# Mixture-of-experts layer: token rows and addresses straight from the tables, scaling parameters on VectorE, and each row gather behind the tile's additions on GpSimd

## The reference

```python
xn = rms_w * (x * rsqrt(mean(x * x) + EPS))
gate_w = softmax(xn @ wg_W + wg_b + (cond @ gg_W + gg_b))
topk_w, topk_i = top_k(gate_w, 2)
cw = sum(one_hot(topk_i, 8) * topk_w[..., None], axis=-2)
h1 = relu(x @ W1[e] + b1[e]); h2 = relu(h1 @ W2[e] + b2[e])
out = x + sum_e cw[..., e] * (h2 @ W3[e] + b3[e])
```

## Time and profile before

| | us |
|---|---|
| median of three runs | 458.6 |
| the profiled execution's own time | 455.86 |
| its span, first to last instruction | 454.2 |
| PE busy | 410.7 |
| POOL busy | 314.9 |
| DVE busy | 304.7 |
| ACT busy | 291.2 |

### The profile page before, as it was taken

One profiled execution on the slowest core, in us unless ns is written; L12 is line 12 of the kernel. 1 busy time (PEld: TensorE's weight loads), 2 busy tenths in 40 slices (PEclk: granted clock), 3 DMA queues, 4 the chain that ended last, 5 costly groups with the idle time before them and its releaser, 6 DMA issues.

```text
span 454.2 us, 12827 instructions
## 1 busy us (share of the span) xinstructions
PE 410.7 (90%) x4110; PEld 365.2 (80%) x4110; DVE 304.7 (67%) x539; ACT 291.2 (64%) x617; POOL 314.9 (69%) x457
## 2 busy tenths in 40 slices
PE   8705989979999989989989989989999999999993
PEld 6505978868888878878878878878888899988892
DVE  4799774858858748748747748655566677776661
ACT  6704959869779668859758855545545556565542
POOL 5631861778678878878778778778878776654534
PEclk9955899999999999999999999999999999999999
DMA  8999289677736737435437435536455444512322
GB/s 299 335 262 338 108 286 375 178 163 189 184 60 165 180 66 168 76 58 78 84 55 183 76 58 81 86 54 105 89 80 86 87 73 71 72 39 36 48 30 31
DMA packets 60968, 57.82 MB, mean 127 GB/s; under 512 B 42059, under 2 KB 55437, under 8 KB 58733
## 3 DMA queue, kind: packets, MB, share of 16 engines
q1 hardware_dynamic: 43072, 38.85, 29.6%
q0 software_dynamic: 13632, 18.00, 24.4%
q10 hardware_dynamic: 4205, 0.17, 0.5%
HBM read 40.08 MB, written 17.83 MB: 128 GB/s over the span
## 4 chain that ended last, share of the span: by engine, by line
POOL 31%; PE 24%; issue 18%; DMA 9%; DVE 6%; POOLq 5%; ACT 5%; SPq 2%; DVEq 1%; ACTq 0%
PE bank L1373 17%; POOL out L688 11%; PE y_banks L1456 5%; POOL area L653 4%; POOL cw L676 3%; DMA out<-in_x 3%; POOL cfrom L648 3%; DMA out<-area,cto 3%; POOLq L664 2%; ACT area L858 2%; POOLq L674 2%; DMA stage<-in_weights 2%; PE bank L1353 2%; POOL cto L648 1%; ACT w_hi L764 1%
## 5 line engine op out<-in xcount | busy, mean ns | idle before, releaser
L1373 PE MATMUL bank<-area,w_hi 128*128 128x256 f16 x1296 | 214.5, 273 | 8.1 <-DVE area L1158 6.6
L1373 PE MATMUL bank<-area,w_lo 128*128 128x256 f16 x648 | 176.6, 273 | 0.0
L872 ACT ACTIVATE area<-bank,cprm 128x256 f32<-128x256 f32 (+1 forms) x264 | 129.4, 558 | 51.3 <-PE bank L1373 32.3
L688 POOL DMA_INDIRECT out<-area,cto x71 | 122.0, 1718 | 44.5 <-issue 15.6
L1156 DVE CAST area<-area 128x512 f16<-128x512 f32 (+1 forms) x144 | 67.2, 467 | 118.3 <-ACT area L872 109.8
L1373 PEld LDWEIGHTS bank<-area,w_hi 128*128 (+1 forms) x1296 | 125.9, 98 | 24.6 <-issue 10.1
L1158 DVE TENSOR_TENSOR area<-area 128x512 f16<-128x512 f32 (+1 forms) x144 | 100.7, 699 | 4.9
L1456 PE MATMUL y_banks<-w_hi,area 128*128 (+1 forms) x520 | 90.8, 273 | 5.5 <-DVE area L1158 5.3
L653 POOL DMA_INDIRECT area<-x_ext,cfrom x65 | 68.2, 1050 | 37.8 <-POOL cfrom L648 28.0
L884 ACT ACTIVATE area<-area,cw 128x256 f32<-128x256 f32 x71 | 32.2, 499 | 65.3 <-DVE area L1163 42.0
L1456 PE MATMUL y_banks<-w_lo,area 128*128 (+1 forms) x260 | 70.9, 273 | 0.0
(11 more groups left out here) (216 smaller groups left out, 504.6 us busy)
## 6 DMA issues: line engine op xcount, KB each, us to landing
stage<-in_weights SPq DMA_DIRECT2D x10, 1024.0 KB, 5.3
area<-in_x SPq DMA_DIRECT2D x8, 512.0 KB, 7.1
x_ext<-in_x SPq DMA_DIRECT2D x8, 512.0 KB
out<-in_x SPq DMA_DIRECT2D x8, 512.0 KB, 10.2
w_lo<-in_weights SPq DMA_DIRECT2D x4, 1024.0 KB, 6.7
w_hi<-in_weights SPq DMA_DIRECT2D x2, 1024.0 KB
out<-area,cto POOLq DMA_INDIRECT x71
area<-x_ext,cfrom POOLq DMA_INDIRECT x65, 3.4
```

What stands on the lines that cost most here:

```text
L688: pool.indirect_dma_start(out=out, out_offset=bass.IndirectOffsetOnAxis(ap=cto[:, s, u:u + 1].bitcast(U32), axis=0), in_=yb[:, s, u, :], i ...
L872: ins = act.activation(to[:, m * T + u * wide:m * T + (u + 1) * wide], ps_h[layer][b][:, a * T + u * wide:a * T + (u + 1) * wide], ACT.Rel ...
L1373: ins = nc.tensor.matmul(out_m, weight, moving, start=(k == 0 and n == 0), stop=(k == chunks - 1 and n == 2))
```

## The change

1. POOL's `copy_columns` is gone: gathers read their offsets from `tab_from`, additions theirs from `tab_to`, with no copy and no wait for one.
2. `parameters(e)` is moved from POOL to DVE, with 12 instructions in place of 14, behind `finish(i)` and `low_parts` of the same steps; rank 0's stands before `x_low(0)`. POOL waits for it through `s_params`.
3. In POOL's turn `gather_into` stands behind `add_rows(i)`, and `copy_weights` stays ahead.
4. At the start POOL issues the gathers of tiles 0 and 1 before it waits for rank 0's parameters; PE transposes tile 1's rows ahead of `layer2(0)`, with 16 filling matmuls in place of 24; ACT's `x_high(1)` stands before `squares(3)`; DVE's `x_low(1)` stands before the second `low_parts(0)`, and `experts_of_tiles` inside step 0, behind its two splits.
5. `low_parts` of chunks 2 and 3 stand in DVE's steps 0 and 1 (before: 1 and 2), behind `finish`; the loads of chunks 8 and 9 follow a step earlier.

```diff
-LOWS_AT, SQUARES_AT, SUMS_AT, HIGHS_AT, PARAMETERS_AT = {1: 2, 2: 3}, {}, {0: 1}, {0: 2, 1: 3}, {0: 1}
+LOWS_AT, SQUARES_AT, SUMS_AT, HIGHS_AT, PARAMETERS_AT = {0: 2, 1: 3}, {}, {0: 1}, {0: 2, 1: 3}, {0: 1}
...
+        def last_rank(i):
+            return 0 if i < FIRST else min(i * E // LEAST, E - 1)
...
-            def copy_columns(to, table, i, signal):
-                pool.tensor_copy(to, table[:, bass.ds(i * SUB, SUB)]).then_inc(signal, 1)
...
+            def gather(i):
+                s = i % RING
                 for u in range(halves_of(i)):
+                    rows = tab_from[:, i * SUB + u:i * SUB + u + 1]
...
             def copy_parameters(i, s):
                 experts = []
+                pool.wait_ge(s_params, last_rank(i) + 1)
...
             def gather_into(n):
-                s = n % RING
                 wait_free(n - RING)
-                copy_columns(cfrom[:, s, :], tab_from, n, s_cfrom)
-                pool.wait_ge(s_cfrom, n - RING + 1)
+                pool.wait_ge(s_cw, n - RING + 1)
                 pool.sem_inc(s_own, 1)
-                gather(n, s, cfrom[:, s, :])
+                gather(n)
...
-            def step(i, s, first=False, late=None, next2=True):
-                copy_columns(cto[:, s, :], tab_to, i, s_idx)
+            def step(i, s, first=False, next2=True):
                 if next2 and i > 1:
                     copy_weights(i + 2, (s + 2) % RING, experts_of[i + 2])
-                for n in GATHERS_AT.get(i, ()):
-                    gather_into(n)
-                pool.wait_ge(s_idx, i + 1)
...
                 add_rows(i, s)
                 if by_halves(i):
                     next_parameters(i, s)
+                for n in GATHERS_AT.get(i, ()):
+                    gather_into(n)
                 if i < 2:
                     copy_weights(i + 2, (s + 2) % RING, experts_of[i + 2])
-                if late is not None:
-                    link(parameters(late))
...
             for i in range(RING):
-                gather(i, i, tab_from[:, i * SUB:(i + 1) * SUB])
-                if i == 0:
-                    pool.wait_ge(s_whole, 1)
-                    pool.wait_ge(s_order, 1)
-                    link(parameters(0))
+                if i == RING - 1:
                     experts_of.append(copy_parameters(0, 0))
+                gather(i)
...
+            def parameters(e, label):
+                dve.wait_ge(s_wsc, e + 1)
+                dve.wait_ge(s_whole, 1)
+                dve.wait_ge(s_b3[e], 16)
+                link(dve.scalar_tensor_tensor(one, w1_sq, xmax4, whole[:, bass.ds(label, 1)], ALU.mult, ALU.add))
+                link(dve.scalar_tensor_tensor(two, one, w2_sq, whole[:, bass.ds(label + E, 1)], ALU.mult, ALU.add))
...
+                ins.then_inc(s_params, 1)
```

More of the change, by code:

```diff
@@ L118 @@
 FLOOR_P = 1.5 * 2.0 ** 23 * P
+WHOLE = 1.5 * 2.0 ** 23
 QUAD = 4
@@ L580, in _ @@
             ins.then_inc(s_iota, 1)
[L582 to L606, removed]
             def inverse_rms(c):
@@ L645, in wait_free @@
                 pool.wait_ge(s_xp if i < BY_PE else s_xs, i + 1)
-            def copy_columns(to, table, i, signal):
-                pool.tensor_copy(to, table[:, bass.ds(i * SUB, SUB)]).then_inc(signal, 1)
-            def gather(i, s, rows):
+            def gather(i):
+                s = i % RING
                 for u in range(halves_of(i)):
+                    rows = tab_from[:, i * SUB + u:i * SUB + u + 1]
                     pool.indirect_dma_start(
                         out=xg[:, s, u, :], out_offset=None, in_=x_ext,
-                        in_offset=bass.IndirectOffsetOnAxis(ap=rows[:, u:u + 1].bitcast(U32), axis=0),
+                        in_offset=bass.IndirectOffsetOnAxis(ap=rows.bitcast(U32), axis=0),
                     ).then_inc(s_xg[s], 16)
@@ L688, in add_rows @@
                     pool.indirect_dma_start(
-                        out=out, out_offset=bass.IndirectOffsetOnAxis(ap=cto[:, s, u:u + 1].bitcast(U32), axis=0),
+                        out=out, out_offset=bass.IndirectOffsetOnAxis(
+                            ap=tab_to[:, i * SUB + u:i * SUB + u + 1].bitcast(U32), axis=0),
                         in_=yb[:, s, u, :], in_offset=None, bounds_check=N - 1, oob_is_err=False,
@@ L750, in _ @@
             for i in range(TILES):
-                step(i, i % RING, first=(i == 0), late=PARAMETERS_AT.get(i),
-                     next2=i + 2 < TILES)
+                step(i, i % RING, first=(i == 0), next2=i + 2 < TILES)
             pool.wait_ge(s_add, MOST * 16)
@@ L910, in _ @@
             activate(0, 0, 0)
+            x_high(1)
             squares(3)
-            x_high(1)
             for i in range(TILES):
@@ L1191, in step @@
                     split(i + 1, 0)
+                if i == 0:
+                    experts_of_tiles()
                 if next1 and two(i) and two(i + 1):
@@ L1204, in step @@
                     copy_weights(LAST, 0, i - AFTER)
-                if late is not None:
+                if late is not None and i >= FRONT:
                     low_parts(late)
@@ L1210, in step, with label_of @@
                     finish(i, s)
+                if late is not None and i < FRONT:
+                    low_parts(late)
+                if i in PARAMETERS_AT:
+                    parameters(PARAMETERS_AT[i], label_of(PARAMETERS_AT[i]))
+            def label_of(e):
+                return dve.value_load(order[0:1, e:e + 1], min_val=0, max_val=E - 1)
+            def parameters(e, label):
+                one, two = bound[:, e, 0:1], bound[:, e, 1:2]
+                w1_sq, w2_sq = fsq[:, e, 0:1], fsq[:, e, 2:3]
+                c1, c2, c3 = (prm[:, e, c:c + 1] for c in range(3))
+                s1, s3, s2, sh1, sh2 = (scale[:, e, c:c + 1] for c in range(5))
+                inv_s1, inv_s3, inv_s2, inv_sh1, inv_sh2 = (inv_scale[:, e, c:c + 1] for c in range(5))
+                dve.wait_ge(s_wsc, e + 1)
[3 more added lines that the diff above has]
+                link(dve.scalar_tensor_tensor(two, one, w2_sq, whole[:, bass.ds(label + E, 1)], ALU.mult, ALU.add))
+                link(dve.tensor_scalar(bound[:, e, :], bound[:, e, :].bitcast(I32), -0.5 * 2.0 ** -MANT, 1.5 * BIAS,
+                                       ALU.mult, ALU.add))
+                link(dve.tensor_scalar(expo[:, e, 3:5], bound[:, e, :], WHOLE, WHOLE, ALU.add, ALU.subtract))
+                dve.tensor_scalar(scale[:, e, 3:5].bitcast(I32), expo[:, e, 3:5], float(TOP_LOG), 2.0 ** MANT,
+                                  ALU.add, ALU.mult)
+                link(dve.tensor_scalar(inv_scale[:, e, :].bitcast(I32), expo[:, e, :], -2.0 ** MANT,
+                                       (2.0 * BIAS - TOP_LOG) * 2.0 ** MANT, ALU.mult, ALU.add))
+                dve.scalar_tensor_tensor(c1, sh1, inv_sx, inv_s1, ALU.mult, ALU.mult)
+                dve.scalar_tensor_tensor(c2, sh2, inv_sh1, inv_s2, ALU.mult, ALU.mult)
+                dve.tensor_tensor(c3, inv_sh2, inv_s3, ALU.mult)
+                for at, sh in ((0, sh1), (KM, sh2)):
+                    ins = dve.tensor_tensor(prm[:, e, 4 + at:4 + at + KM],
+                                            packed[:, bass.ds(label * (2 * KM) + (KH + KH * E + at), KM)],
+                                            sh.to_broadcast([P, KM]), ALU.mult)
+                ins.then_inc(s_params, 1)
@@ L1212, in _ @@
             dve.wait_ge(s_sx, 1)
             dve.sem_inc(s_y32, 1)
+            first_label = label_of(0)
             low_parts(0, (0,))
+            parameters(0, first_label)
             x_low(0)
@@ L1217, in _ @@
             split(0, 0)
+            x_low(1)
             low_parts(0, (1,))
-            x_low(1)
             tables()
-            experts_of_tiles()
             for i in range(TILES):
```

11 lines of the change are left out of this document (4 added, 7 removed).

## The result

The changed kernel takes 460.35 us (median of 20 runs, 458.89 to 464.36) beside 457.55 for the kernel before (20 runs, 447.72 to 461.0): 2.8 us or 0.6% more. The ratio reported for this comparison is 1.0219, interval 1.0162 to 1.0276; it rests on the two lowest of the 20 runs before alone, 447.72 and 453.69 (that of experiment 10 likewise on the four lowest of 23), so the medians are the fairer reading. A second comparison on another chip gave 459.81 (12 runs) beside 457.25 (23 runs) and a ratio of 1.0061, interval 1.0033 to 1.0089. The forecast was 461.3 us, 2.7 above its base of 458.6, with a range of 455 to 468; the result lies in it, and the change of the medians, 2.8, is as large as the forecast's 2.7.

A forecast was written before the change was run, and what follows sets the result against it. POOL was taken to bound the kernel from tile 4 to tile 22. 454.2 + 12.0 (ring) - 9.9 (gain) + 0.6 (VectorE's parameters) = 456.9, 2.7 longer; on the median 458.6 becomes 461.3 us, range 455 to 468.

The forecast's parts named there:

- ring: Turns 0 to 2: weigh(i), additions(i), gather(i+4), landing, x_high(i+4), weigh(i+1) wait on each other; costs 12.0 us by tile 4.
- The gain from tile 4 to tile 22: With parameters and column copies out of POOL's turn, PE runs at its own pace there; 9.9 us less.
- lap: One pass from weigh(i) through additions, second gather and its landing to x_high(i+4); 11.54 us, ends 10.5 and 14.
- VectorE's parameters: 12 small DVE instructions behind finish, 1.8 us long; 0.1 us per rank from rank 2 on, 0.6 in all.
- the second rival: TensorE's clock falls in PE's gaps of the early laps; 2.2 us per slow stretch, 463.5 or 465.7; chance 0.30.
- The start: Tile 0's weigh(0) comes 1.3 us earlier, 73.4 in place of 74.73, as experts_of_tiles moves; counted inside the 12.0.
- VectorE shutting GpSimd out: VectorE's casts block POOL's additions and gathers behind weigh; 0.9 us in each early lap, 2.7 more, forecast 464.0.
- The first rival: Gathers of tiles 4 to 6 land before ACT needs them, so the kernel is faster, about 449; chance 0.10.
- The third: Gathers from tile 7 on land late too, delaying x_high up to tile 19; six times 1.5 us, about 470; chance 0.15.

The follow-up runs named there:

- experiment 10: The changed kernel with 40 filling matmuls ahead of layer 3 of tile 4 alone: 458.69 us beside 457.25 for the kernel before, ratio 1.0128.
- experiment 1: The changed kernel with all gathers ahead of the wait for s_y and the additions again: 442.04 us beside 456.13 for the kernel before, ratio 0.9703.
- experiment 3: The changed kernel with gathers still behind the additions, but tiles 4, 5 and 6 gathered one turn earlier: 443.56 us, ratio 0.9732 to the kernel before.
- Experiment 8: The changed kernel with gathers ahead of the additions in every turn but turn 2: 446.81 us, ratio 0.9776 to the kernel before.
- experiment 6: The kernel before with the column copies dropped and parameters still on POOL: 448.89 us beside 456.93, ratio 0.9812.
- Experiment 4: The changed kernel with 40 filling matmuls ahead of layer 3 of tiles 2, 3 and 4: 458.0 us beside 456.13 for the kernel before, ratio 1.0051.
- experiment 5: The kernel before with one edit, gathers behind the additions: 485.39 us beside 456.93, ratio 1.062.
- experiment 2: The changed kernel with gathers ahead of the additions in turns 0, 1 and 2 alone: 443.42 us, ratio 0.9705 to the kernel before.

## Why the prediction was right, point by point

The mechanism came as forecast: ring, gain behind it, and the order of their sizes. That the number fits so well, 2.8 us for 2.7, is partly luck. Against the profiled execution, on which the sum was built, the change is 4.3 us in span; the clock's 2.8 us were missing in the sum, and the other three terms were 1.4 too high together. The medians hide this, since the kernel before was profiled in an execution 1.7 us below its median.

- **The ring**: forecast 12.0 us, measured 11.4 at tile 4. Each of its times came within 0.7 us. Experiments 1 and 3 take it away in two ways, by order and by distance, and both bring the stretch from tile 0 to tile 4 from 59.0 to 43.6 us. That is 15.4: the kernel before had lost 2.9 there already, and 1.05 is the earlier start. Experiment 8 measures one lap, 11.37. The additions of the second lap were longer than the 1.7 each that I took (2.03 and 2.06), and the landing shorter than 3.7: used 2.9 us after issue. The two errors cancelled. PE's idle time was forecast as 4 to 6 us in each lap; it was 4.66, 1.79 and 5.49. In the second lap PE was late from the slow clock before and had less to wait for.
- **The gain from tile 4 to tile 22**: forecast 9.9, measured 10.1 (199.41 less the 189.34 of experiment 1; in the changed kernel 7.3 is left of it, as the clock takes 2.8). PE has no idle time behind tile 5. ACT's wait for POOL's copy of the parameters is gone from the list.
- **VectorE's parameters**: forecast 1.8 us long, 0.6 us in all. They run as this timeline of DVE's step 3 shows, and the split behind them still waited 0.43 for ACT, so they cost nothing; the earlier trace rows had the gap of 1.96 that they fill. From tile 4 to tile 22 experiment 1, with the parameters on VectorE, and experiment 6, with them on POOL, take the same 189.34 and 189.35 us:

```profile
119.30 0.74 DVE L1131 SCALAR_TENSOR_TENSOR area<-y_banks,cprm 128x512 f32<-128x512 f32 x1
119.96 0.21 DVE L1199 SCALAR_TENSOR_TENSOR bound<-fsq,small 128x1 f32<-128x1 f32 x1
...
121.59 0.23 DVE L1212 TENSOR_TENSOR prm<-packed,scale 128x4 f32<-128x4 f32 x2
122.24 0.56 DVE L1124 CAST area<-area 128x512 f16<-128x512 f32 x1 [0.43 <-ACT area L840]
```

- **The clock**: the second rival, to which I gave 0.30, came about beside the forecast. Its price was 2.8 us in the profiled execution (2.2 worked out from the stretch at 0.81). It had the right place: the fall in the first lap had cover, the one behind the last had none. Experiment 4 shows the cover: tile 3 was 2.2 us late and tile 4 was not. The term belonged into the sum; with it the forecast would have been 463.5, further from the median and nearer in what it adds to the profiled execution, whose span grew by 4.3 and not 2.7. The rule of the Trainium skill that the prediction cites (TensorE: Matmul & The Clock Gate, What's actually happening), that the gate goes by how busy the engine has been recently, agrees: 84.90 to 89.40 and 118.40 to 123.77 are idle, and the fall came in each.
- **The start**: weigh(0) 1.05 us earlier (73.68 for 74.73), forecast 1.3.
- **VectorE shutting GpSimd out**: the 2.7 us given for it beside the sum did not appear in full. The six additions of the three laps took 11.3 us together where 10.2 were forecast, and the longest of the whole trace took 2.15; whether VectorE lengthened them no run tells. The prediction also misread its own row: beside the addition of 2.53 us (116.52) VectorE ran `low_parts` (L932, 116.28 to 118.75) and then `finish`, no copy or cast, so that row doesn't bear on the rule.
- **One wait not foreseen**: in the first lap PE stood not ahead of layer 3 but ahead of the small matmul of the weight sums, which needs ACT's squares, and these stand behind `x_high(4)`:

```profile
89.49 0.59 PE L1278 MATMUL bank<-wsq,ones 128*128 128x3 f32 x2 [4.66 <-ACT wsq L758]
```

Layer 1 of tile 3 and layer 3 of tile 2 followed at the low clock, so tile 2 started at 95.01 where 89.4 + 3.25 = 92.7 would be due. It had cover up to weigh(2).

- **The first rival** (the ring doesn't bind, faster, about 449) fell. The third (late gathers throughout) fell for this kernel, and experiment 5 shows it in the kernel before, where POOL's turn is longer. How much is to spare at later tiles the trace of the changed kernel tells. The tightest is tile 12, its second gather and its `x_high`:

```profile
173.05 0.98 POOL L628 DMA_INDIRECT area<-x_ext,tab_from  x1 [0.30 <-issue]
```

```profile
180.37 0.72 ACT L814 ACTIVATE xr<-area,small 128x512 f16<-128x512 f32 x1
```

It comes 7.32 us after the issue, where the waiting ones of the three laps came 2.8 to 2.9 after it; so some 4.4 us were to spare, and 3.3 were forecast.

Experiments 1, 2 and 3 beat both kernels, with 442.0, 443.4 and 443.6 us. The rest of the change, without its third point, gains 14 us.

## What to carry to other kernels

When a fetch is moved behind a result in an in-order queue, look for the shortest distance in turns between a fetch and its use, usually in the first few turns, and add up the lap: if the consumer stands ahead of the next result on its own engine, the lap closes and each such turn lasts as long as the lap. Reliefs of one engine don't add up once the next engine is the bound; here either of two was nearly enough. A gap in TensorE's work can be paid twice: here gaps of 3.1 to 5.5 us brought the clock to 0.50, and the slower matmuls behind the last gap cost 1.4 to 2.8 us more, since nothing covered them.

## What the runs showed that was not expected

The kernel before with the gathers behind the additions lost 28 us (ratio 1.062), more than twice the changed kernel's ring: a queue that is already the bound pays for the same move far beyond the first turns. And the length of the low clock behind one and the same gap (5.49 us long both times) differed between executions of the same kernel, 6.8 and 3.4 us, with a price of 2.8 and 1.4. Either of two reliefs alone gave the whole of the later gain.
